# Scores of both attention passes contracted over 32 rows in row strips of TensorE

## The reference

```
x = L0_attn_x                       # (8, 512, 128) float32
xn = layernorm(x)
q, k, v = split(xn @ w_attn)        # 16 heads of 8 channels
scores = q @ k.T / sqrt(8) + causal_mask - log1p(decay[h] * log1p(dist))
y = softmax(scores) @ v
out = x + y @ w_proj + sum over the top 2 of 8 experts of gate * (silu(xn @ W1[e].T) @ W2[e].T)
```

## Time and profile before

| | us |
|---|---|
| median of 3 runs | 771.75 (770.9 to 772.74) |
| profiled execution, span | 769.8 |
| TensorE busy (PE) | 648.5 |
| weight loads (PEld) | 427.1 |
| VectorE busy | 494.0 |
| GpSimd busy | 435.7 |
| ScalarE busy | 312.7 |

### The profile page before, as it was taken

One profiled execution on the slowest core, in us unless ns is written; L12 is line 12 of the kernel. 1 busy time (PEld: TensorE's weight loads), 2 busy tenths in 40 slices (PEclk: granted clock), 3 DMA queues, 4 the chain that ended last, 5 costly groups with the idle time before them and its releaser, 6 DMA issues.

```text
span 769.8 us, 14013 instructions
## 1 busy us (share of the span) xinstructions
PE 648.5 (84%) x4380; PEld 427.1 (55%) x4381; DVE 494.0 (64%) x1115; ACT 312.7 (41%) x399; POOL 435.7 (57%) x295
## 2 busy tenths in 40 slices
PE   0392716999999899999899999998799999999950
PEld 0191415565665556666566656664376766767630
DVE  8618504887778677877678777786344544545535
ACT  3560003556555455555456555556222222222210
POOL 5210773686777667777577877787133333434332
PEclk9999856999999999999999999999699999999985
DMA  9920210021111111110111111013511111111119
GB/s 202 168 100 14 66 52 21 19 51 29 36 39 39 28 42 33 28 50 26 32 45 28 49 27 37 26 26 124 144 39 49 52 48 50 47 46 54 53 61 280
DMA packets 48299, 45.40 MB, mean 59 GB/s; under 512 B 6878, under 2 KB 38368, under 8 KB 47984
## 3 DMA queue, kind: packets, MB, share of 16 engines
q1 hardware_dynamic: 43888, 36.14, 19.4%
q0 software_dynamic: 4352, 8.47, 3.4%
HBM read 17.13 MB, written 17.44 MB: 45 GB/s over the span
## 4 chain that ended last, share of the span: by engine, by line
PE 80%; DVE 10%; another core or an unknown queue 3%; issue 2%; DMA 2%; POOL 1%; SPq 0%; ACT 0%; DVEq 0%; POOLq 0%
PE ps L1072 13%; PE psO L1145 11%; PE ps L1237 10%; PE ps L1115 10%; PE ps L1218 8%; PE ps L1227 4%; PE ps L1075 4%; PE psM L1027 4%; PE psM L1057 3%; PE ps L1118 2%; PE psM L1058 2%; PE psM L1043 2%; DVE neg_max L934 2%; PE psO L1034 2%
## 5 line engine op out<-in xcount | busy, mean ns | idle before, releaser
L464 POOL TENSOR_TENSOR probs<-probs,wdist 128x1024 f32<-128x1024 f32 (+1 forms) x124 | 275.5, 2226 | 110.8 <-ACT probs L709 110.5
L934 DVE TENSOR_REDUCE neg_max<-ps 128x1 f32<-128x512 f32 (+3 forms) x448 | 214.7, 531 | 99.5 <-PE ps L1075 79.1
L709 ACT ACTIVATE probs<-ps 128x1024 f32<-128x1024 f32 x160 | 163.9, 1025 | 155.0 <-PE ps L1118 118.1
L1072 PE MATMUL ps<-k_heads,q_rows 128*128 128x512 f32 (+3 forms) x512 | 141.5, 369 | 39.5 <-DVE neg_max L934 33.8
L650 POOL DMA_INDIRECT picked_dram<-values,k_heads x72 | 70.7, 982 | 129.9 <-DVE values L1001 126.9
L1072 PEld LDWEIGHTS ps<-k_heads,q_rows 128*128 128x128 f32 x512 | 88.5, 199 | 86.2 <-issue 49.0
L1115 PE MATMUL ps<-q_rows,k_heads 128*128 128x384 f32 (+3 forms) x512 | 119.4, 345 | 0.0
L745 ACT ACTIVATE probs<-ps 128x512 f32<-128x512 f32 x72 | 43.0, 597 | 144.9 <-PE ps L1218 144.9
L1145 PE MATMUL psO<-probs,values 128*32 128x512 f32 (+3 forms) x1024 | 97.3, 453 | 3.6 <-DVE probs L462 3.5
L1237 PEld LDWEIGHTS ps<-wdist,probs 128*128 128x128 f32 x576 | 70.6, 193 | 31.6 <-issue 31.2
L1075 PE MATMUL ps<-mask_q,ident_bf 128*128 128x256 bf16 (+1 forms) x320 | 86.2, 269 | 0.0
(11 more groups left out here) (157 smaller groups left out, 701.1 us busy)
## 6 DMA issues: line engine op xcount, KB each, us to landing
k_heads<-k_rows SPq DMA_DIRECT2D x128, 64.0 KB
rows_dram<-probs SPq DMA_DIRECT2D x1, 4680.0 KB, 36.2
k_heads<-rows_dram SPq DMA_DIRECT2D x72, 65.0 KB, 1.8
probs<-picked_dram SPq DMA_DIRECT2D x8, 512.0 KB, 7.4
send_rows<-xn_all SPq DMA_DIRECT2D x32, 65.5 KB, 1.9
wdist<-w1t SPq DMA_DIRECT2D x2, 1024.0 KB
out<-x_all SPq DMA_DIRECT2D x8, 256.0 KB, 5.1
xt_dram<-probs SPq DMA_DIRECT2D x6, 256.0 KB, 2.1
```

Of the source, the lines that this page charges most:

```text
L464: return eng.tensor_tensor(part, part, weights, ALU.mult)
L709: nc.scalar.activation(probs[:, at.ring(2), w, :], ps2[:, (at.c * P2_UNITS + w) % 2].rearrange("p a b -> p (a b)"), ACT.Exp).then_inc(exp_ ...
L934: last = nc.vector.tensor_reduce(dst, src, AX.X, ALU.max, negate=True)
L1072: mm(dst[:, 0:n], q[:, tile * P:n], k[:, quad, 0:n], start=first, stop=False)
```

## The change

A score matmul takes only the 32 partitions of its head, of `k_rows` and of `q_rows`; which quarter of the array's rows it uses follows from the partitions. `k_heads`, its memsets, its DMAs and their semaphore go; `k_rows` becomes a ring of four; the expert part's row buffers get memory of their own. The first pass has 12 units in six pairs: both units of a pair are the same tile (or tiles 2 and 0) of two neighbouring heads. In a pair both banks are waited for, then both score matmuls are issued, then both masks. Tile 1 has one head per bank, so VectorE has four reduces of 256 columns where two of 2x256 were. The second pass has six parts; the last two hold tile 2 of two heads each, in half of each of two banks, and ScalarE has two exponentials of 2x256 columns for one of 1024. In a slot the steps `P1` 10 to 12 and `P2` 5 are added at the end.

```diff
-P1_UNITS = 10
-P2_UNITS = 5
+P1_UNITS = 12
+P2_UNITS = 6
...
     step("P1", n, NGROUP, 8, 10)
     step("NT", n - 4, NGROUP)
     step("P2", n - 2, NGROUP, 4)
+    step("P1", n, NGROUP, 10, 12)
+    step("P2", n - 2, NGROUP, 5)
...
-        k_rows = sb("k_rows", [P, 2, SEQ], F32R)
-        k_heads = [sb(f"k_heads{r}", [P, QUADS, SEQ], F32R) for r in range(4)]
+        k_rows = sb("k_rows", [P, 4, SEQ], F32R)
...
-                sp.wait_ge(zeroed, 4)
...
-                    for quad in range(QUADS):
-                        rows = slice(quad * QROWS, (quad + 1) * QROWS)
-                        sp.dma_start(k_heads[at.ring(4)][rows, quad, :].bitcast(F32),
-                                     k_rows[rows, at.ring(2), :].bitcast(F32)).then_inc(k_loaded, 16)
...
-                for t in k_heads:
-                    nc.gpsimd.memset(t[:].bitcast(F32), 0.0).then_inc(zeroed, 1)
...
+                        out = probs[:, at.ring(2), 4, (w - 4) * 512:(w - 3) * 512]
+                        nc.scalar.activation(out.rearrange("p (a b) -> p a b", a=2), ps2[:, w % 2, :, 0:256],
+                                             ACT.Exp).then_inc(exp_ready, 1)
...
+                        kind, q = u % 6 // 2, 2 * (u // 6) + u % 2
+                        todo = {0: [(bank[:, 0:512], neg_max[:, r, 3, q:q + 1])],
+                                1: [(bank[:, 0:384], neg_max[:, r, 2, q:q + 1]),
+                                    (bank[:, 384:512], neg_max[:, r, 0, q:q + 1])],
+                                2: [(bank[:, 0:256], neg_max[:, r, 1, q:q + 1])]}[kind]
...
+                    first, kind = 2 * (u0 // 6), u0 % 6 // 2
+
+                    def scores(unit, tile, col, start=True):
+
+                        rows = slice((first + unit) * QROWS, (first + unit + 1) * QROWS)
                         n = (tile + 1) * P
-                        mm(dst[:, 0:n], q[:, tile * P:n], k[:, quad, 0:n], start=first, stop=False)
...
+                        mm(ps1[:, unit, col:col + n], q_rows[rows, at.ring(4), tile * P:n],
+                           k_rows[rows, at.ring(4), 0:n], start=start, stop=False)
...
-                        pe.wait_ge(k_loaded, at.groups(64, 64))
...
+                    for unit in range(2):
+                        if at.looped or at.c * P1_UNITS + u0 + unit >= 2:
+                            pe.wait_ge(p1_free, at.groups(P1_UNITS, u0 + unit - 1))
+                        scores(unit, 3 - kind, 0)
+                    for unit in range(2):
+                        if kind == 1:
+                            scores(unit, 0, 384, start=False)
+                    for unit in range(2):
+                        mask(unit, (384, 256, 128)[kind], (1, 2, 1)[kind])
...
+                        for s in range(2):
+                            rows = slice((2 * (w % 2) + s) * QROWS, (2 * (w % 2) + s + 1) * QROWS)
+                            last = mm(pair[:, s, col:col + SEQ - a], k_rows[rows, at.ring(4), a:a + P],
+                                      q_rows[rows, at.ring(4), a:], start=start, stop=w >= 4)
```

More of the change, by code:

```diff
@@ L351, in build @@
         send_rows = [sb(f"send_rows{r}", [P, TOKEN_ROW]) for r in range(2)]
[L353 to L354 removed]
+        slot_rows_all = sb("slot_rows", [P, RING, ROW])
+        slot_rows = [slot_rows_all[:, j, :] for j in range(RING)]
         slot_xt, slot_y8 = (values[:].rearrange("p a t h r -> p (a t h r)")[:, a:a + n * P].rearrange(
@@ L962, in dw_step @@
                             dve.wait_ge(exp_ready, at.groups(P2_UNITS, TILE_UNITS[tile][-1] + 1))
-                            for w in TILE_UNITS[tile]:
+                            for w in TILE_PARTS[tile]:
                                 last = apply_decay(nc.vector, at, w, tile)
@@ L1074, in mask @@
-                    def mask(dst, blocks):
-                        return mm(dst, ident_bf[:], mask_q[:, 0:blocks * P], start=False, stop=True)
+                        mm(ps1[:, unit, col:col + n], q_rows[rows, at.ring(4), tile * P:n],
+                           k_rows[rows, at.ring(4), 0:n], start=start, stop=False)
+                    def mask(unit, col, blocks):
+                        mm(ps1[:, unit, col:col + blocks * P], ident_bf[:], mask_q[:, 0:blocks * P], start=False,
+                           stop=True).then_inc(p1_full, 1)
@@ L1109, in p2_step, with scores @@
                         pe.wait_ge(exp_ready, at.groups(P2_UNITS, w - 1))
[L1110 to L1112 removed]
+                    pair = ps2[:, w % 2]
+                    def scores(tile, col, start=True):
                         a = tile * P
[L1115 to L1133 removed]
+                        for s in range(2):
+                            rows = slice((2 * (w % 2) + s) * QROWS, (2 * (w % 2) + s + 1) * QROWS)
+                            last = mm(pair[:, s, col:col + SEQ - a], k_rows[rows, at.ring(4), a:a + P],
+                                      q_rows[rows, at.ring(4), a:], start=start, stop=w >= 4)
+                        return last
+                    if w < 2:
+                        scores(0, 0)
+                    elif w < 4:
+                        scores(1, 0)
+                        scores(3, 384, start=False)
+                    else:
+                        last = scores(2, 0)
+                    if w < 4:
+                        for s in range(2):
+                            last = mm(pair[:, s, 0:P], ident_bf[:], mask_k[:], start=False, stop=True)
                     last.then_inc(p2_full, 1)
```

81 lines of the change are left out of this document (14 added, 67 removed).

## The result

| | before | after |
|---|---|---|
| median of 4 runs, us | 771.33 (770.56 to 772.74) | 881.75 (877.22 to 894.27) |
| profiled execution, span | 769.8 | 892.4 |
| mean granted TensorE clock | 0.945 | 0.851 |
| first to last copy of the heads' outputs | 147.1 to 544.4 | 153.1 to 663.2 |

The ratio is 1.141 (95%: 1.1356 to 1.1464): 110 us slower, where 44 were forecast, and outside the range. The clock's record begins at 83.8 us in before and at 148.2 us in after. Ahead of it the mean in the table counts the clock as full, although TensorE's records there have the lengths of 1.2 GHz (masks of 128 columns take 0.39 us up to 146 us in after, and 0.28 from 148.95 on). So both means are too high, after's by more.

The account below looks back on a forecast made before the run. TensorE's queue in the attention stage was taken as the bound. +1.32 us a group times 32 gave +42 us; with 2 us for early reduces, 44 on the median of 771.75 made 816 us, range 758 to 842.

Parts of the forecast that it names:

- The stage and its bound: All edited steps lie in the attention stage, where TensorE's queue sets a group's cost, 12.8 us on average.
- Strips side by side: In score matmuls, two heads in two row strips stream at once: a pair of 512 columns takes 0.22 us.
- (d): Score pairs: loads of two row strips run one after the other, +1.6 us a group, 867 us; chance 0.11.
- A price for each change of shape: Between strips and full array TensorE stands empty: entering a strip step costs 0.21 us, leaving to the masks 0.12.
- (b): Score steps: no price for row strips but longer waits, -0.2 us a group, 766 us (755 to 773); chance 0.17.
- (c): Score steps: a price for shape changes on one side only, or half, 773 to 795 us; chance 0.08.
- The two waits: At the slot's end TensorE waits for VectorE's reduces: 0.90 us before units 10 and 11, 0.73 before 0 and 1.
- The sum: Score steps per group: 6.90 us of work plus 1.63 of waits less the present 7.21, +1.32 us; times 32, +42.
- (a): Score steps as worked out, with the column strips' price and both waits: 816 us, 795 to 842; chance 0.60.
- Edits at the side: Other engines: VectorE and ScalarE additions fit idle time, key transfers and GpSimd's memsets give nothing, extra early reduces cost 2 us.
- The 2 us beside the indirect transfers: Until 116.5 us, extra VectorE reduces beside GpSimd's indirect transfers cost 0 to 6 us, taken as 2.
- (e): TensorE's clock falls to 1.2 GHz, from waits or half the array used; a third of the stage: 80 us; chance 0.04.

Follow-up runs that it names:

- r1: The changed kernel's twelve units, order and waits, but score matmuls contract over all 128 rows of zero-padded key copies again; 803.67 us, 1.0619 of before.
- r6: r1 with each mask issued as four matmuls of 32 output rows, all 128 rows in use; 856.68 us, 1.1327 of before.
- r11: r9 with each mask as two matmuls in the score's own 64-row strip and the key copies' zeros written later; 758.43 us, 0.9842 of before.
- r7: The changed kernel with 64-row strips (32 of them zeros), heads 0 with 2 and 1 with 3 paired, key copies back; 814.06 us, 1.078 of before.
- r10: The changed kernel with useless work: output transposes done three times, those of the maxima twice; 831.2 us, 1.0877 of before.
- r2: The changed kernel, 32-row strips kept, with a slot's steps reordered so other TensorE work lies between first-pass pairs; 875.22 us, 1.1531 of before.
- r9: r7 with its steps in r8's order; 776.36 us, 1.0055 of before.
- r8: r1 in another order, with value products and projections put between two pairs of the first pass; 764.69 us, 1.0114 of before.
- r12: The kernel before with the four key-copy memsets issued behind GpSimd's two layer normalisation steps; 771.67 us, 1.0002 of before.
- r13: r11 with the four output transposes issued twice; 768.97 us, 0.9962 of before.

## Why the prediction was wrong, by its own steps

**The stage and its bound.** Right. The edited steps decide, and TensorE's queue is what a group costs.

**Strips side by side.** Right: the pair of 512 columns takes 0.49 us for 0.71 in r1. Rival (d) falls with it.

**A price for each change of shape.** Right in kind, and taken from the right rows, but a little high (see the sum below). Loads in after, idle before in brackets:

```profile
214.13 0.18 PEld L1056 LDWEIGHTS ps<-k_rows,q_rows 32*128 32x128 f32 x1
214.55 0.11 PEld L1060 LDWEIGHTS ps<-mask_q,ident_bf 128*128 128x128 bf16 x2 [0.24 <-issue]
214.77 0.18 PEld L1093 LDWEIGHTS ps<-q_rows,k_rows 32*128 32x128 f32 x2
```

Row strips pay as column strips did. The cited rule of "TensorEngine Tiling (Array Packing)" in the Trainium skill, that a change of mode drains TensorE, holds for them too; r6 puts the price of a change in and out at some 0.2 us and r11's masks save it. Rivals (b) and (c) fall.

**The two waits.** Right in place, kind and size. VectorE beside the rows of after at 2.4 GHz:

```profile
211.27 1.42 DVE L921 TENSOR_REDUCE neg_max<-ps 128x1 f32<-128x384 f32 x4 [0.47 <-PE ps L1060]
...
213.32 0.76 DVE L921 TENSOR_REDUCE neg_max<-ps 128x1 f32<-128x256 f32 x2
```

The four reduces end at 212.69 and unit 11's load starts at 212.74. Part 4's columns end at 211.71+0.38-0.17 = 211.92, so the pair of units 10 and 11, 0.11 us of columns, would have ended at 212.03 without a wait; it ends at 212.74+0.38-0.17 = 212.95: 0.92 us for the forecast's 0.90. Unit 10 goes ahead at 212.08, as soon as its own bank is free, but that wins nothing, because the masks behind it need unit 11. Ahead of the next slot, part 5's columns end at 213.27+0.39-0.17 = 213.49 and the pair's 0.22 would end at 213.71; it ends at 213.80+0.83-0.17 = 214.46: 0.75 for 0.73. Together 1.67 for 1.63.

**The sum.** Too high by 0.24 us a group, and that lies in the steps between the waits. Units 2 and 3 with part 1, in the same slot:

```profile
216.75 0.40 PE L1045 MATMUL psM<-k_lo,k_lo_to 128*128 128x512 f32 x1
...
218.26 0.28 PE L1106 MATMUL ps<-mask_k,ident_bf 128*128 128x128 bf16 x2
```

From the end of the columns ahead (216.98) to the end of their own masks (218.37) they take 1.39 us, where the forecast has 0.78+0.66 = 1.44. All score steps from 214.68 to 228.70, read in this way and with their waits, take 8.31 us for the forecast's 6.90+1.63 = 8.53, and 8.31-7.21 = 1.10 agrees with the measured +1.08. The twenty changes of a group together cost some 0.25 us less than the column strips' rows had them. So of the 42 us forecast for the groups, the part at the full clock came to 33. Two slips of the forecast's arithmetic change nothing: the terms of (a) reach down to 790 and not 795, where (c) stands in any case, and (d)'s sixteen loads of 0.11 us are 1.8 a group and not 1.6.

**Edits at the side.** "Nothing" for GpSimd's memsets was wrong in its size: they held VectorE for 5.7 us. The rows read were GpSimd's, and the engine beside it wasn't read. It decided nothing. The 2 us beside the indirect transfers can't be told apart from the rest of the 6.0 at the start.

**The clock.** This is the step that failed. Rival (e) named it, with two possible causes in one sentence, priced it ("a fall in a third of the stage would add 80 us") and gave it 0.04, because the present stage is at 1.00 throughout. But that row shows a stage in which every matmul runs on all rows. It is no evidence for one in which pairs use 64 of them. The change takes away half of the 4.3 us a group that score columns streamed on all rows, and has the other half stream on 64. The fall came for 225 of 510 us and cost some 79. These 225 us hold some 146 us of work at the full clock, a third of the stage, so (e)'s price for such a fall came out as it stood; that it took just a third as its case is luck, since nothing in the prediction says how far the fall would go. Of the two causes named, the waits are refuted by r1, and the half of the array, here the rows in use, is shown to be it by r7, which has the same pairs and waits, and by r10, which adds work on all rows and raises the clock. Orders that cover the waits say the same: r2 with pairs on 64 rows has 1.1531 and r9 with pairs on 128 has 1.0055. The third suspect, the changes of shape, is refuted by r6. What amount of work on the array keeps the clock up isn't shown.

The Trainium skill would not have decided it: "TensorE: Matmul & The Clock Gate", Part 1, describes the clock as following how busy TensorE has recently been. Here TensorE is busy for 45.00 of 45 us at 0.51 in one row and for 48.45 of 50 at 1.00 in r1's. Busy time as the profile counts it doesn't tell the two apart, so the measurement goes beyond the page.

Had (e) stood in the sum as a term of unknown size, with nothing at one end and at the other the whole stage at the low clock, the range would have been open upwards and would have held 882. That the direction was right rests on the steps that were worked out: at the full clock after would be 33 us slower still.

## What to carry to other kernels

Splitting TensorE into strips paid here only where the strips that run together fill the rows: with two of 64, half of them zeros, the clock was low for 9% of the stage (4% in a better order), with two of 32 for 44%. A step that takes the full array between two strip steps costs some 0.2 us for going and coming back, so masks that add to a strip's result belong in the same strips; and a pair needs other work behind it that covers both its reduces. All three together turned 1.141 into 0.984. When a change uses less of the bottleneck engine than before, its clock is a term of the sum with both ends, however steady the clock is in the trace of before.

## What the runs showed of the hardware that was not expected

- TensorE busy without a gap was granted 1.2 GHz (45 of 45 us, clock 0.51) when its score pairs used 64 of 128 rows; with all rows, and more gaps, 2.4 GHz.
- The zeros count as rows in use: r7's added rows hold nothing but zeros and brought the low stretches from 225.3 to 41.0 us. What is left of them was not separated; in r8's order they are 17.1 us, all of it behind the stands named below.
- Useless transposes on all rows made a kernel faster, 1.0877 for 1.141 (by the medians 1.099 for 1.143).
- Some of what is left of the low clock stands behind idle time of TensorE where a round of the loop ends: 2.5 us in before and then 3.4 us low, 3.1 us in r9 and then 13.7 us low. Not each such stand lowers it.
- A GpSimd memset of 7 us held a VectorE operation on 16 columns for 5.88 us that takes 0.17 without it.
- The kernel before itself took 756 us on two chips and 771 on a third. The kept traces show the difference ahead of the first copy: beside the indirect transfers and up to 145 us, VectorE has gaps of over 3 us that sum to 23 to 28 us in before, after, r9, r11, r12 and r13, and to 0 to 8 us in the other profiles. What makes them on the one chip isn't shown.
